# A two-layer LSTM-aggregation GNN on one core: gathering x rows for every step instead of rows of a precomputed gate table

## The reference, cut to what matters

```python
def _lstm_last(seq, wih, whh, bih, bhh):            
    def step(carry, x_t):
        h, c = carry
        g = x_t @ wih.T + h @ whh.T + (bih + bhh)
        i, f, gg, o = split(g, 4)
        c = sigmoid(f) * c + sigmoid(i) * tanh(gg)
        h = sigmoid(o) * tanh(c)
        return (h, c), None
    ...

def _sage_conv(x, src, ...):
    msgs = x[src].reshape(512, 33, 128)
    return _lstm_last(swapaxes(msgs, 0, 1), ...) @ wl.T + bl + x @ wr.T

h = relu(_sage_conv(x, src, conv1...))
out = _sage_conv(h, src, conv2...)
x = layernorm(x + out)
hr = einsum('ni,rio->rno', x, weight)
msg = hr[edge_type, src] * edge_weight[:, None]
x = layernorm(x + relu(segment_sum(msg, dst)))
```

## Time and profile before

| | us |
|---|---|
| median of 3 runs | 576.14 |
| lowest and highest run | 573.68, 580.67 |
| span of the profiled execution | 570.4 |
| PE busy in it | 485.2 (85%) |
| DVE busy | 399.5 (70%) |
| ACT busy | 325.8 (57%) |
| POOL busy | 309.4 (54%) |

### The profile page before, as it was taken

One profiled execution on the slowest core, in us unless ns is written; L12 is line 12 of the kernel. 1 busy time (PEld: TensorE's weight loads), 2 busy tenths in 40 slices (PEclk: granted clock), 3 DMA queues, 4 the chain that ended last, 5 costly groups with the idle time before them and its releaser, 6 DMA issues.

```text
span 570.4 us, 9783 instructions
## 1 busy us (share of the span) xinstructions
PE 485.2 (85%) x3463; PEld 349.4 (61%) x3463; DVE 399.5 (70%) x1114; ACT 325.8 (57%) x832; POOL 309.4 (54%) x320
## 2 busy tenths in 40 slices
PE   8766998979897999778897888887899987978795
PEld 4644786757676785656666766775785543444343
DVE  5544887858676895557776776876787975757665
ACT  4734766737556674545565665655675664545543
POOL 6476565665546501676664566666204655656551
PEclk9997999979999999978989999999999999999899
DMA  5665665675646502665665456556202111111111
GB/s 191 204 188 168 180 192 159 177 195 161 175 125 197 166 11 93 187 180 161 172 169 148 134 163 183 167 169 181 77 1 79 48 38 38 42 38 41 39 42 29
DMA packets 28346, 72.85 MB, mean 128 GB/s; under 512 B 6795, under 2 KB 10691, under 8 KB 28298
## 3 DMA queue, kind: packets, MB, share of 16 engines
q0 software_dynamic: 20768, 64.77, 40.0%
q1 hardware_dynamic: 6442, 6.54, 4.0%
q10 hardware_dynamic: 1088, 0.92, 0.5%
HBM read 69.05 MB, written 3.16 MB: 127 GB/s over the span
## 4 chain that ended last, share of the span: by engine, by line
PE 39%; DVE 17%; ACT 16%; another core or an unknown queue 13%; issue 8%; DMA 6%; POOL 1%; DVEq 0%; ACTq 0%; POOLq 0%
PE gates L1254 18%; DMA edge_rows<-msg_table,msg_index 6%; PE gates L1247 5%; PE work L1254 4%; DVE msg_full L1090 3%; ACT act_if L601 3%; ACT h_hi L597 3%; DVE prod_fc L906 2%; DVE prod_ig L908 2%; ACT msg_full L750 2%; PE work L1247 2%; DVE h_full L877 2%; ACT act_o L619 2%; ACT tanh_c L593 2%
## 5 line engine op out<-in xcount | busy, mean ns | idle before, releaser
L524 POOL DMA_INDIRECT rows<-gate_table,src_steps x226 | 224.7, 994 | 165.1 <-issue 64.5
L1247 PE MATMUL gates<-ident,rows 128*128 128x128 f32 x686 | 99.5, 281 | 39.5 <-issue 20.8
L601 ACT ACTIVATE act_if<-gates 128x512 f32<-128x512 f32 x113 | 67.8, 600 | 104.1 <-remote 54.5
L539 POOL DMA_INDIRECT edge_rows<-msg_table,msg_index x76 | 75.5, 993 | 79.6 <-DMA msg_table<-table_sb 30.9
L1254 PE MATMUL gates<-h_hi,whh_hi 128*128 128x256 f16 x396 | 104.7, 283 | 13.1 <-ACT h_hi L597 6.6
L906 DVE TENSOR_TENSOR prod_fc<-act_if,cell 128x256 f32<-128x256 f32 x128 | 54.2, 424 | 81.3 <-issue 37.3
L1247 PEld LDWEIGHTS gates<-ident,rows 128*128 128x128 f32 x686 | 78.1, 144 | 52.1 <-issue 49.7
L1254 PE MATMUL gates<-h_hi,whh_lo 128*128 128x256 f16 x396 | 104.1, 281 | 0.0
L1254 PE MATMUL gates<-h_lo,whh_hi 128*128 128x256 f16 x396 | 88.1, 282 | 0.4 <-issue 0.4
L890 DVE TENSOR_TENSOR h_lo<-h_full,h_hi 128x256 f16<-128x256 f32 x128 | 54.2, 423 | 12.3 <-ACT h_hi L597 0.9
L1080 DVE TENSOR_SCALAR rows<-node_iota,dst_f 128x512 f16<-128x512 f16 x132 | 43.4, 365 | 26.8 <-ACT msg_full L750 25.7
(11 more groups left out here) (186 smaller groups left out, 800.5 us busy)
## 6 DMA issues: line engine op xcount, KB each, us to landing
rows<-gate_table,src_steps POOLq DMA_INDIRECT x226
gate_table<-rows SPq DMA_DIRECT2D x8, 256.0 KB
edge_rows<-msg_table,msg_index POOLq DMA_INDIRECT x76
code<-code_table SPq DMA_DIRECT2D x6, 160.0 KB
msg_table<-table_sb SPq DMA_DIRECT2D x4, 192.0 KB, 2.4
code<-code_table SPq DMA_DIRECT2D x5, 128.0 KB
whhT<-turned_whh SPq DMA_DIRECT2D x2, 256.0 KB
wihT<-turned_wih ACTq DMA_DIRECT2D x1, 256.0 KB, 2.9
```

The source lines that it names most:

```text
L524: pool.indirect_dma_start(rows[:, j * K + k, :], None, gate_table[l], bass.IndirectOffsetOnAxis(src_steps[:, t, k:k + 1], axis=0)).then_in ...
L539: pool.indirect_dma_start(edge_rows[:, c % 2, n, :], None, msg_rows, bass.IndirectOffsetOnAxis(msg_index[:, pool_first(c) + n:pool_first(c ...
L601: act.activation(act_if[:, h, :], gates[:, h, 0, :], ACT.Sigmoid, scale=1 / G_SCALE).then_inc(if_ready[h], 1)
L1247: pe.matmul(gate_place(t, h, gate)[:, k * P:(k + 1) * P], rows[:, j * K + 2 * h + k, gate * P:(gate + 1) * P], ident[:, :], is_transpose=True,
```

## The change

Which step gets its input how is now a string for each layer, `MODES`: "X" is rows of x gathered and turned by PE, "P" is picked by one-hot, "G" would be the table. The changed kernel has no "G".

- All 33 steps of layer 0 and steps 2 to 32 of layer 1 are "X": POOL gathers four tiles of 128 rows x 512 bytes from `x` (layer 0) or from a new DRAM tensor `h1_table` (layer 1) into a ring of five steps (`x_rows`); PE turns them (`turn_rows`, in step t-1, between the input parts of the two halves); ACT and DVE write `xg_hi`, `xg_lo` (128x512 each, f16); PE makes 24 products a step with them (`gathered_part`).
- Steps 0 and 1 of layer 1 stay picked by one-hot ("P").
- Nothing of the tables is left: no `project`, `add_bias`, `table_part`, no stores of tables. Between the layers DVE copies the turned h1 to `h1_rows` and SP stores them (two stores of 128 KB); POOL waits for both stores.
- The one-hots are built from the source indices as int32, broadcast by one DMA to all partitions (2 x 512 numbers each, 512 KB in all) instead of by PE and ACT (`spread_src`, `take_src` go).
- At the start 18 instead of 9 warming matmuls; the loads of `xT`, `x_nodes` and of the indices are issued by SP after the rows of steps 0 and 1 of layer 0 have been turned.
- Step 1 of layer 0 loses its own order (`recurrent_ahead`, `picked_last`) and runs like the others. The matmul that puts `xT_biased` into `turned_bank[0]` moves from step 23 of layer 1 to behind its last step.

```diff
-DIRECT = (1, 2, 12)
-HALF = 21
+STEPS = 33
+MODES = ("X" * STEPS, "PP" + "X" * (STEPS - 2))
...
+    DEEP, XDEEP = 5, 5
...
+    SLOTS = DEEP * K if by_rows else 12
...
+            for l, t in fetched:
+                if (l, t) == (0, 2):
+                    pool.wait_ge(src_loaded, 16)
+                by_x_row = MODES[l][t] == "X"
+                if by_x_row:
+                    turn = by_x.index((l, t))
+                    if turn >= XDEEP:
+                        pool.wait_ge(rows_turned, 2 * (turn - XDEEP + 1))
+                    if l == 1 and by_x[turn - 1][0] == 0:
+                        pool.wait_ge(h1_stored, 32)
...
+                    at = issued.index((l, t, k))
+                    if at >= UNDER_WAY:
+                        pool.wait_ge(*landing(*issued[at - UNDER_WAY]))
...
+            def take_x(l, t):
+                i = x_turn(l, t)
+                if MODES[l][t] == "X":
+                    act.wait_ge(rows_turned, 2 * (by_x.index((l, t)) + 1))
+                    act.activation(xg_hi[:, i % 2, :], row_bank[i % 2], ACT.Copy, scale=X_SCALE).then_inc(xg_hi_ready, 2)
...
+                    if 0 < t < T - 1 and of_x(l, t + 1):
+                        take_x(l, t + 1)
...
+            def take_x(l, t):
+                if MODES[l][t] == "X":
+                    dve.wait_ge(xg_hi_ready, 2 * (i + 1))
+                    dve.scalar_tensor_tensor(xg_lo[:, i % 2, :], row_bank[i % 2], X_SCALE, xg_hi[:, i % 2, :],
+                                             op0=ALU.mult, op1=ALU.subtract).then_inc(xg_lo_ready, 2)
...
+            def turn_rows(l, t):
+                bank = row_bank[x_turn(l, t) % 2]
+                for k in range(K):
+                    pe.wait_ge(*landing(l, t, k))
...
+                    mm = pe.transpose(to, x_rows[:, x_slot(l, t, k), :], ident[:, :])
...
+                    input_first(t, 0)
+                    input_second(t, 0)
+                    if t + 1 < T and MODES[l][t + 1] == "X":
+                        turn_rows(l, t + 1)
+                    input_first(t, 1)
+                    input_second(t, 1)
                     recurrent(t, 0, l * (T - 1) + t)
                     recurrent(t, 1, l * (T - 1) + t)
...
+            for h in range(2):
+                sp.wait_ge(h1_rows_ready, h + 1)
+                sp.dma_start(h1_table[h * HN:(h + 1) * HN, :].rearrange("(k p) c -> p k c", p=P),
+                             h1_rows[:, 2 * h:2 * (h + 1), :]).then_inc(h1_stored, 16)
```

462 lines of the change are left out of this document (183 added, 279 removed).

## The result

| | before | after |
|---|---|---|
| median us | 574.94 (4 runs) | 611.48 (4 runs) |
| lowest and highest | 573.68, 580.67 | 608.02, 620.56 |
| span of the profiled execution | 570.4 | 607.7 |
| PE busy | 485.2 (85%) | 530.2 (87%) |

The ratio after to before is 1.0593, 95% interval [1.0506, 1.0681]: about 37 us slower, where the forecast was 20 us faster and its range ended at 592.

The account below looks back on a forecast made before the run. The prediction took late PE signals under gather traffic as the bound, then PE at 5.67 us a step. -22.1 + 3.5 + 4 - 6.2 + 0.4 = -20.4 from 576.1 gave 555.7 us; range 546 to 592.

Parts of the forecast that it names:

- What bounds the kernel before: Whole kernel: no one busy engine; steps lose 1.6 us each, some 95 us in all, with DMA traffic.
- Late signals of PE: Slow steps: act_if starts well after PE's products are recorded, under heavy gather traffic; 54.5 us of such waits.
- PE per step, 5.67 us: Steps 2 to 32, both layers: 52 matmuls at 0.109 us make PE the limit; -22.1 us before late signals.
- D: Rival, every step: the loop or DVE's side work shows through, 0.2 us a step, +12, 568 us; chance 0.11.
- Late signals, "+0.06 a step": Steps 2 to 32, both layers: late signals nearly gone, 0.06 us a step left, 3.5 us in all.
- POOL per step, 5.04 us, "hidden": Every step: four 64 KB gathers at 1.26 us each, hidden as long as they stay under 5.67 us.
- Rival C: Every step: POOL becomes the limit when a gather takes over 1.42 us; at 1.5, +20, 576 us; chance 0.08.
- Start, 28.8, then +4: Start of layer 0: act_g of step 2 at 28.8 us (before 28.59), then SP's burst of loads costs +4 us.
- Boundary, -6.2: Between layers, act_g of step 32 to act_g of step 2: 30.3 us before, 6.2 less, bounds -2 and -9.
- End, +0.4: Behind the last step: one more f32 matmul (xT_biased), +0.4 us (0 to 0.4); edge phase unchanged.
- B: Rival, every step: late signals stay, from gather number or PE's instruction stream, not bytes; 600 to 648 us; chance 0.13.
- the stretch 98 to 108: Kernel before: DMA share 0.53, gathers at full count, steps under 5 us; cited against late signals staying.

Follow-up runs that it names:

- e2: Changed kernel with the same 256 gathers, each carrying 128 bytes of a row instead of 512; 616.2 us.
- e15: Kernel before with three gathers of gate rows a step instead of four, PE's work kept; 521.1 us against 587.6 on the same chip.
- e5: Changed kernel with SP issuing the same transfers as plain loads of rows in order and POOL issuing nothing in the layers; 544.9 us.
- e6: Changed kernel with POOL issuing plain loads of 128 rows in order instead of gathers by index; 545.2 us.
- e11: Changed kernel with SP loading the rows and POOL writing eight lists of 512 numbers a step instead of gathers; 546.3 us.
- e1: Changed kernel with only the first ring of 20 gathers issued and its tiles read again by later steps; 552.2 us.
- e3: Changed kernel with two gathers a step instead of four, each tile turned twice so PE's work is the same; 555.0 us.
- e17: Changed kernel with its ring growing within a layer from two steps to five, output unchanged; 630.8 us, ratio 1.0764 to the kernel before.
- e18: Changed kernel with POOL writing a list of 768 numbers ahead of each step's four gathers, as a pause; 614.0 us, ratio 1.069.
- e8: Changed kernel with three gathers a step instead of four, the fourth tile turned from the first one's rows; 580.8 us.
- e9: Changed kernel with POOL waiting for the gather before to land at each of three turns after a layer's first; 626.8 us.

## Why the prediction was wrong

**What bounds the kernel before.** "Late signals of PE" was the right finding, and 1.6 us a step, 95 us in all, about the right size: with two gathers a step the kernel before takes 88 us less. The step that failed is the sentence after it, that they "come under heavy gather traffic", taken as bytes. The number of gathers stood in the same rows: POOL (x0) in the quiet stretch, x105 and x102 in the layers. e2 (a quarter of the bytes, the same loss) and e15 (the same traffic, three gathers, 1.1 us less a step) show that it isn't the bytes; e5, e6 and e11 show that of POOL's work only the indexed gathers do it, as far as was tried.

**PE per step, 5.67 us.** Right to a hundredth: 5.68 in the quiet steps and in e1, e3, e5, e6 and e11. ACT and DVE hide behind it, as costed; D didn't come.

**Late signals, "+0.06 a step".** The mis-sized term. The sum has 3.5 us for steps 2 to 32 of both layers; measured are 194.4 + 177.7 = 372.1 us against 340.2, so 31.9. Of these about 15 are the one stall in (0,2), the rest is the steady state: 6.08 to 6.09 against 5.68, 0.4 a step, some 20 us for 50 steps, about all of the gain. It isn't today's 1.6 us either: the step is held at 6.05 in both kernels, by POOL's four gathers and a pause, so that what PE saves or adds under that value doesn't count. This is why layer 1 is nearly equal (-1.1): the change could win nothing in a step, whatever it did to PE, as long as four gathers a step stay.

**POOL per step, 5.04 us, "hidden".** The price was right (1.25 a gather), the word hidden was wrong. Rival C asked from which price on POOL is the limit by its own time and put it at 1.42; the limit comes with about 1 us of pause a step on top.

**Start, 28.8, then +4.** Measured 36.02 for (0,2). In e5 it is 26.35 with the same burst of SP's loads, and the fill is 34.2 instead of 57.7: the burst that I priced at 4 us costs nothing, and all of the loss at the start, 9.7 us up to (0,2) and 15.4 in step (0,2), goes with the gathers. The forecast had no term for the ring's filling, here or at the boundary, and that is the larger part of the miss: 20 gathers from 27.4 to 52.7 in one run, none of them needed before (0,3). The kernel before fills its ring there too, with steps of 12.4 and 13.2 us.

**Boundary, -6.2.** +16.0. Without gathers of POOL it is 23.4, where I had 24.1. The 22.9 us between go with POOL's run of 24 gathers (239.6 to 269.9), which begins beside the picking, two steps ahead of its need.

**End, +0.4.** The part that the change touches is right: the first gather of the edge phase comes 12.3 us behind act_g of (1,32), against 12.8 before. The edge phase itself took 3.4 us longer; over the 18 runs that loop varies from 122.5 to 128.8 us with no relation to the edits, so I give these 3.4 us no cause.

**The rivals.** B was the case that came, with its cause rightly named as one of two ("they go with the number of gathers") and a chance of 0.13. Its argument against, that the stretch 98 to 108 has steps under 5 us at full count, didn't weigh: the unevenness of steps in the kernel before (4.3 to 8.8) is that of POOL's runs. Its thresholds were also set too high: the sum without late signals is 552.2, so from (576.1 - 552.2) / 60 = 0.40 us a step on the kernel is no faster, not from 0.47, and from 0.59 on it is over 2% slower, not from 0.66. The steady loss measured, 0.4, stands right at the first. And the price was too narrow: it spread today's loss evenly over the steps and had no term for a stall that lasts as long as the ring takes to fill. The Trainium skill's rule on instruction fetch (Runtime: NRT & Kernel Launch, instruction fetch mechanics), that it is mostly hidden, agrees with the runs: e1, with the same program, has no late signal to speak of. The trace also speaks against gathers that hold up PE's fetches: of the 33 packets of 16 KB on the instruction queue (q8) none lies in either stall. The next ones start at 61.4 and 273.8, when PE already works again (from 55.7 and 272.8), and take 0.96 and 0.93 us, no longer than those of e1 (0.9 to 1.5).

**The clock.** In the stalls the granted clock falls to 0.50, the lower level (1.2 GHz), after PE has stood still; it costs its share at the end of a stall (19 matmuls in the 3.0 us from 274.0 at a clock of 0.60). It follows the stall and doesn't make it: in e17 it is 1.00 in the 6.5 us before PE slows and 0.70 after, and in the two stretches of e18 it is 1.00 with PE at half of its rate.

**The signals or PE itself?** PE's ends are modelled, so its records could be early instead of its signals late. The semaphore events that the trace holds decide it for the steady state. PE's signal for the turned rows and its next one lie 18 matmuls apart in its program. Over the 34 steps of the table's "step" they arrive 2.18 us apart in every step of e1, e3, e5, e6, e8 and e11, but under 0.5 us apart, mostly 0.22, in 33 of the 34 steps of the changed kernel and in 30 of e2. 18 matmuls at 0.109 take 1.96 us and don't fit into 0.22. So they had been done when the first signal came, and it was the signal that was held back.

**Open.** Why POOL's gathers hold PE's signals back isn't shown by any run. In the stall of layer 0 PE also issues single matmuls 2 to 3 us apart (48.0, 50.1, 52.9) with no wait that the trace names; whether that has the same cause is open. Nor do I know why breaks of 0.96 us leave PE at half rate in the fills of e18, when breaks hardly longer (0.96 to 1.16 us of idle time) leave it at 93% in the steady state of the changed kernel.

## What to carry to other kernels

Before an edit that gives PE more work "behind" POOL's indexed gathers, count the gathers a step and add a pause: here 4 x 1.25 + 1.05 = 6.05 us was the floor of a step for two quite different kernels with rings of five, and only fewer gathers moved it down (three: 4.9 to 5.1, two: 4.6 to 4.7). Don't let such gathers run far ahead of their use: the time in which a ring fills is largely taken from PE. And when a loss appears with a resource in one stretch and not in another, list everything else that differs between the two before naming it; one run with a quarter of the bytes would have decided it.

## What the runs showed of the hardware that I had not expected

- In long runs of indexed gathers that POOL issues 1.25 us apart, PE all but stops: 12 matmuls in 8.6 us (e17, after 6.5 us at nearly the full rate), 4 in 7.9 (changed kernel), one in 9.9 (e9). ACT and DVE, which wait for its signals, stop too, and PE then waits for them.
- The semaphore signals of PE's matmuls can come long after the matmuls: 2.8 us after the record in steady steps of the changed kernel, some 20 us in its stall of layer 1.
- It doesn't depend on bytes: 128-byte rows (share of the DMA queues 0.14) and 2,048-byte rows (0.54) are both hit.
- 256 plain loads by SP or by POOL (0.54 us each), and 267 us of list writing by POOL leave PE's steady steps at 5.68 us, to the hundredth. List writing isn't free for DVE: six one-hots beside it took 4.49 us instead of 2.46.
- The granted clock over the whole span goes with it: 0.955 in the changed kernel, 0.988 with SP's loads.
